# W1 and the vectors wait for the first group of x; VectorE takes over that group's moments

## What is computed

```python
h = jnp.maximum(_layernorm(x, axis=-1), 0.0)
# in the layer:
h = inp @ W1 + b1
e = jax.nn.leaky_relu((h @ a1)[:, None] + (h @ a2)[None, :] + b2, ALPHA)
attention = jnp.where(adj > 0, e, jnp.float32(-1000000000000.0))
attention = jax.nn.softmax(attention, axis=1)
h_prime = attention @ h
return x + elu(h_prime)
```

## Time and profile before

| what | value |
|---|---|
| median of 3 runs | 459.96 us (459.87 to 460.02) |
| span of the profiled execution | 458.2 us |
| PE busy | 423.9 us, 93% |
| DVE busy | 387.6 us, 85% |
| ACT busy | 309.1 us, 67% |
| POOL busy | 126.3 us, 28% |
| mean of the DMA traffic | 176 GB/s |

### The profile page before, as it was taken

One profiled execution on the slowest core, in us unless ns is written; L12 is line 12 of the kernel. 1 busy time (PEld: TensorE's weight loads), 2 busy tenths in 40 slices (PEclk: granted clock), 3 DMA queues, 4 the chain that ended last, 5 costly groups with the idle time before them and its releaser, 6 DMA issues.

```text
span 458.2 us, 8873 instructions
## 1 busy us (share of the span) xinstructions
PE 423.9 (93%) x3399; PEld 416.1 (91%) x3399; DVE 387.6 (85%) x388; ACT 309.1 (67%) x297; POOL 126.3 (28%) x155
## 2 busy tenths in 40 slices
PE   0799879788889999999999999999999999999995
PEld 0789879787888899999999999999999999999995
DVE  3999799999998805999999549999996399999915
ACT  2687898777665418995776289958663789586603
POOL 3242289999999940000000000000000000000004
PEclk9999998989899999999999999999999999999999
DMA  8930025554543630754738806656468156566202
GB/s 279 382 132 1 1 92 185 183 185 185 183 176 109 240 118 14 263 199 169 255 158 285 292 21 226 232 183 224 188 237 295 63 191 259 192 208 250 92 0 92
DMA packets 22355, 80.60 MB, mean 176 GB/s; under 512 B 1472, under 2 KB 14016, under 8 KB 14144
## 3 DMA queue, kind: packets, MB, share of 16 engines
q1 hardware_dynamic: 21920, 79.70, 49.0%
q10 hardware_dynamic: 416, 0.66, 0.4%
HBM read 76.15 MB, written 4.19 MB: 175 GB/s over the span
## 4 chain that ended last, share of the span: by engine, by line
PE 67%; POOL 12%; issue 9%; DVE 7%; DMA 2%; POOLq 1%; ACT 1%; SPq 0%; DVEq 0%; ACTq 0%
PE ps L599 39%; PE ps L601 19%; POOL h_raw L325 12%; DVE stats L656 2%; DMA x_s<-x 2%; PE ps L617 1%; PE ps L616 1%; PE ps L615 1%; DVE hnT_lo L683 1%; PE ps L526 1%; DVE h_raw L692 1%; PE ps L528 1%; PE ps L527 1%; DVE y L868 1%; DVE xn L673 1%
## 5 line engine op out<-in xcount | busy, mean ns | idle before, releaser
L599 PE MATMUL ps<-hp_hi,w_hi 128*128 (+1 forms) x960 | 240.5, 288 | 12.7 <-POOL hp_lo L328 12.5
L601 PE MATMUL ps<-hp_lo,w_hi 128*128 (+1 forms) x960 | 238.1, 285 | 0.0
L730 DVE SCALAR_TENSOR_TENSOR adj_s<-R,p,adj_s 128x1024 f32<-128x1024 f32 x128 | 171.7, 1382 | 38.8 <-ACT adj_s L392 38.8
L599 PEld LDWEIGHTS ps<-hp_hi,w_hi 128*128 128x128 f32 x960 | 184.5, 192 | 17.4 <-issue 12.7
L601 PEld LDWEIGHTS ps<-hp_lo,w_hi 128*128 128x128 f32 x960 | 184.4, 192 | 0.0
L400 ACT ACTIVATE w_hi<-adj_s 128x2048 fp32r<-128x2048 f32 x64 | 122.5, 1913 | 56.0 <-DVE adj_s L730 38.5
L740 DVE SCALAR_TENSOR_TENSOR w_lo<-adj_s,w_hi 128x2048 fp32r<-128x2048 f32 x64 | 153.1, 2394 | 3.7 <-ACT w_hi L400 3.7
L392 ACT ACTIVATE adj_s<-adj_s 128x2048 f32<-128x2048 int32 x64 | 122.2, 1910 | 20.1 <-DMA adj_s<-adj_t 20.1
L599 PE MATMUL ps<-hp_hi,w_lo 128*128 (+1 forms) x960 | 125.2, 283 | 0.6 <-DVE w_lo L740 0.6
L599 PEld LDWEIGHTS ps<-hp_hi,w_lo 128*128 128x128 f32 x960 | 119.5, 189 | 0.8 <-DVE w_lo L740 0.8
L339 POOL TENSOR_TENSOR adj_s<-y,adj_s 128x256 f32<-128x256 f32 x8 | 5.7, 712 | 283.8 <-DVE y L868 283.5
(11 more groups left out here) (88 smaller groups left out, 269.1 us busy)
## 6 DMA issues: line engine op xcount, KB each, us to landing
adj_s<-adj_t SPq DMA_DIRECT2D x64, 1024.0 KB, 4.8
x_s<-x SPq DMA_DIRECT2D x8, 512.0 KB, 10.4
o_s<-x SPq DMA_DIRECT2D x3, 1024.0 KB, 8.5
out<-o_s SPq DMA_DIRECT2D x6, 512.0 KB, 6.9
adj_s<-x SPq DMA_DIRECT2D x1, 1024.0 KB, 5.5
out<-adj_s SPq DMA_DIRECT2D x8, 128.0 KB, 1.7
vec<-vectors ACTq DMA_DIRECT2D x1, 384.5 KB, 6.4
W1x<-W ACTq DMA_DIRECT2D x1, 256.0 KB, 4.4
```

What stands on the lines that cost most here:

```text
L599: last = pe.matmul(acc, block_w, hh, start=False, stop=False)
L601: pe.matmul(acc, block_w, hl, start=False, stop=False)
L730: last = dve.scalar_tensor_tensor(sgn, R[:, ds(ic * CW, CW)], p[:, ds(source(r, c) + s, 1)], sgn, ALU.max, ALU.mult)
```

## The change

ACT loads its table first, then waits for the first group of x, and only then issues the loads of W1 and the vectors. For group 0 alone, DVE turns the raw statistics into mean and variance itself: four `bn_aggr`, and a copy of the means to `mean`. ACT takes the root from `agg`. POOL's `moments` starts at group 1. DVE inverts and normalises group 0 before the statistics of group 1. The semaphore counts of `stat_ready` and `var_ready` go down by one accordingly.

```diff
             def moments(g):
-                pool.wait_ge(stat_ready, g + 1)
+                pool.wait_ge(stat_ready, g)
...
-            for g in range(4):
+            for g in range(1, 4):
                 moments(g)
...
         @block.scalar
         def _(act):
+            act.preload_act_table(ACT.Sqrt)
+            act.wait_ge(x_in[0], 16)
             act.dma_start(W1x[:, :, 0:F], W1.rearrange("(c p) f -> p c f", p=P)).then_inc(w_in, 16)
             act.dma_start(vec[:, :], vectors.partition_broadcast(P)).then_inc(vec_in, 16)
 
             def root(g):
-                act.wait_ge(var_ready, g + 1)
+                act.wait_ge(var_ready, g)
...
-            act.preload_act_table(ACT.Sqrt)
             act.wait_ge(eps_ready, 1)
-            root(0)
+            act.wait_ge(agg_ready, GT)
+            act.activation(std[:, 0:GT], agg[:, :, 1], ACT.Sqrt, bias=eps[:, 0:1]).then_inc(std_ready, 1)
             normalise(0)
...
-                last.then_inc(stat_ready, 1)
+                if g > 0:
+                    last.then_inc(stat_ready, 1)
+                else:
+                    link(last)
+
+            def aggregate():
+
+                for t in range(GT):
+                    dve.bn_aggr(agg[:, t, :], stats[:, 0, t, :]).then_inc(agg_ready, 1)
+                dve.wait_ge(agg_ready, GT)
+                dve.tensor_copy(mean[:, 0:GT], agg[:, :, 0])
...
             statistics(0)
-            statistics(1)
+            aggregate()
             invert(0)
             normalise(0)
+            statistics(1)
             weights()
```

More of the change, by code:

```diff
@@ L134, in build @@
         mom = sb("mom", [P, GROUPS, 4, GT])
+        agg = sb("agg", [P, GT, 2])
         mean = sb("mean", [P, TILES])
@@ L172, in build @@
         var_ready = sem("var_ready")
+        agg_ready = sem("agg_ready")
         std_ready = sem("std_ready")
```

## The result

The changed kernel takes 464.71 us (464.63 to 465.27, 4 runs) against 459.91 for the kernel before on the same chip: a ratio of 1.0109 (95% interval 1.0095 to 1.0123), 4.8 us more. The profiled execution's span is 462.9 us against 458.2. The forecast was slower, by 1.1 us, with 463.1 as the upper end: the way was right, the size was not.

The account below looks back on a forecast made before the run. PE (93% busy) bounds the kernel, and a shift in DVE's preparation passes through in full: `weights()` at 11.7 instead of 10.6 adds 1.1 us, span 459.3, plus 1.8 to the median gives 461.1 us; range 459.6 to 463.1.

Parts of the forecast that it names:

- What sets the end: DVE's own list sets the preparation from 8.32 us; a shift of `weights()` reaches `u` and the end in full.
- x of group 0 earlier: Without W1 beside it, x of group 0 lands at 4.7 us (4.6 worked out) in place of about 5.4.
- DVE's head: DVE's work on groups 0 and 1, `bn_aggr` and copy at 0.5 us, brings it to `weights()` at 9.45, not 10.59.
- The cap on any gain: If the vectors are in time, DVE waits for group 1's root at 11.7; gain 0.7 us, chance 0.13.
- The wait that takes its place: DVE stands at `weights()` from 9.45 until the vectors, issued at 5.3, land at 11.7: 1.1 us later than before.
- Is 6.4 still the right time to landing?: Vectors' time from issue to landing: shortening and lengthening terms taken as balanced, 6.4 us kept; landing bounds 10.8 and 13.8.
- a saving of up to 0.9: If ACT's later issue starts like SP's, 0.9 us are saved and the vectors land at 10.8.
- The 8 KB packets of the adjacency: Three or four of each engine's eight vector packets run beside adjacency packets, making the vectors 0.9 us later.
- ACT's issues are held as SP's are: Rival: ACT's issues block about 1 us longer each, vectors land at 12.7 to 13.8; 462.1 to 463.2, chance 0.13.
- The page's fit: Skill page's DMA time, about 2.0 us plus bytes at 436 GB/s: vectors there at about 8.2, before DVE asks.
- The 16 engines serving two queues in turn: DMA engines serve SP's and ACT's queues packet for packet, 337 and 264 packets while both had work.

Follow-up runs that it names:

- the rest alone: Changed kernel with W1 and the vectors issued at the head of ACT's list again, no wait for x: 460.00 us, ratio 1.0007.
- the hold after two groups: Changed kernel, but SP stops after two groups of x until ACT has issued W1 and the vectors: 459.47 us, ratio 0.9992.
- the kernel with the earlier issue: Changed kernel without ACT's wait for x of group 0, table load still first: 460.36 us, ratio 1.0011.

## Why the prediction was right in its way and wrong in its size

- *What sets the end:* right. The last table shows it over 5.6 us of shifts of `weights()` (9.58 to 15.20): 45.5 us on to `u`, within 0.1, in every kernel where neither group 1's root nor the adjacency came to be waited for in the path, and from `u` to the end 402.0 within 0.3 in all.
- *x of group 0 earlier:* right, a little under-sized: 4.43 against the 4.7 taken and the 4.6 worked out.
- *DVE's head:* right. 0.38 us for four `bn_aggr` and 0.17 for the copy; arrival at `weights()` at 9.02 against 9.45. The cap on any gain (group 1's root) was seen in the run of the rest alone: 0.73 us of waiting, no gain.
- *The wait that takes its place:* the right place and the right load, and this is where the size went wrong. The failing step is "Is 6.4 still the right time to landing?", where the terms that shorten and lengthen were taken as balanced and 6.4 was kept. It has no term for the packets that SP had already issued and that had not yet moved. Measured: 10.2. Of the 3.8 us more:
  - The start. ACT's first packets came 2.0 us behind their issue before, and 4.0 behind it now. The prediction had put a saving of up to 0.9 here, should the later issue start as SP's had. Where little stood ahead, the saving was there: 1.1 us in the hold after two groups, in place of 2.0. In the changed kernel SP had issued 174 packets per engine and 49 of them had gone (790 over 16 engines, at 4.43). That backlog cost 4.0 - 1.1 = 2.9 us, and it is the term that broke the sum.
  - The 8 KB packets of the adjacency. The prediction took 0.9 of at most 2.0 for them. With them moved away the vectors took 8.7 us; with them 10.2. So 1.5 us. The size was near, the way it came about was not: it had them meet three or four of each engine's eight vector packets, late in the transfer, and they met W1's packets, before the first vector packet.
  - The remaining 0.3 us were not taken apart (3.8 = 2.9 - 0.9 + 1.5 + 0.3).
- *The rival "ACT's issues are held as SP's are":* its time, up to 463.2, was nearest, but not by its mechanism. ACT's issues took 0.45 and 0.84 us against 0.50 and 0.52; the root followed at 6.36, undisturbed. The queue ahead was long, not the issue. Holding SP so that it was not blocked (after four groups) helped little: 464.01 us.
- *The page's fit* (2.0 us plus the bytes at 436 GB/s, 8.2 for the landing) was off by 7 us in the changed kernel. In the Trainium skill, "DMA: Bandwidth & Descriptors", section "Anatomy of one DMA", it is given for DMAs that GpSimd issues; these are issued by ACT. With the DMA engines left free behind group 1 both loads were in by 8.6, 4.3 us from W1's issue; the fit for both in turn gives 2.0 + 1.5 = 3.5 (an estimate from the page). So it comes near with engines that are nearly free, and says nothing on loaded ones.

The 16 engines serving two queues in turn, as the prediction took from the earlier trace rows, fits the rows once both have packets at the engine. The Trainium skill, "DMA: Bandwidth & Descriptors", section "Queues, rings and completion order", says that an engine goes round the queue rows that it has work for, and that it drains a whole packet of one row, some 9 to 17 descriptors and at most 64, before it switches. If what the profile counts as a packet is one such descriptor, a turn takes 0.5 to 0.9 us, and 3.4 at most (an estimate from the page's figures and the 300 per us over 16 engines of the earlier trace rows). The 1.1, 2.4, 3.0 and 2.9 us of waiting over W1's own start lie above the usual turn and below the longest. No run here shows how long a turn is, so the rule neither gives the size nor is refuted. The measurement says this much: a newly issued load starts later the more of the other queue's packets stand ahead. How deep that stock is at most (the three longest waits show 116 to 130 gone per engine, with 46 to 58 of them later than 1.1 us behind W1's issue, an estimate of when it could have begun) and where it sits was not settled.

## What to carry to other kernels

A small load that everything needs is safe when it is issued before the big ones, even if it slows the first of these down by 1 us: moved behind them, it stands behind much of what is queued before it shares with the rest. If it has to come later, keep the queue ahead short: with two groups of x ahead the cost was gone (459.47 us), with three it was 1.2 us, with four 4.1. Do not carry over a time to landing from an empty queue to a full one; count what stands ahead at the moment of the new issue, and of what size its packets are. And before a wait is put ahead of a load for the sake of another, read how much the consumer has to spare (here 2.9 us), and set against it how much later the load will land: the later issue and the queue ahead together (here 7.4 us).

## What the hardware showed that I had not expected

- ACT's DMA issue did not wait for a table load that stands ahead of it in ACT's list: in the kernel with the earlier issue W1 was issued at 0.75, while the load ran from 0.72 to 2.00.
- The adjacency's packets of 8 KB cost a load on the other queue 1.5 us without meeting it: they slowed W1, which stood ahead of the vectors on ACT's queue.
- Four `bn_aggr` on 128x6 took 0.38 us together, less than the 1.6 us that POOL's seven small operations took for the same four tiles (6.92 to 8.49 before).
